# Setup loads moved from ScalarE's queue to SyncE's, and the own rows' factor of the second layer's softmax carried in scalars

## The chip, the cores and the metric

The kernel runs on one core of a Trainium2 chip. The metric is the device time of one execution in microseconds. The kernel before takes 4919.24 us (median of three runs, 4918.93 to 4925.36). One more execution was profiled; it took 4916.51 us, and its trace is the one read here.

## The reference

Four graph layers run one after the other over 6250 nodes of 256 numbers and 106250 edges sorted by target node. Each layer norms x, takes the positive part, does its own work and adds the result to x.

```python
edge_index = jnp.stack([src, dst])
h = jnp.maximum(_layernorm(x, axis=-1), 0.0)
x = x + _L0_gnn_ref(h, L0_gnn_weight, L0_gnn_bias, edge_index, edge_weight)
h = jnp.maximum(_layernorm(x, axis=-1), 0.0)
x = x + _L1_gnn_ref(h, edge_index, L1_gnn_W, L1_gnn_b, ...)
h = jnp.maximum(_layernorm(x, axis=-1), 0.0)
x = x + _L2_gnn_ref(h, edge_index, L2_gnn_W, L2_gnn_a)
h = jnp.maximum(_layernorm(x, axis=-1), 0.0)
x = x + _L3_gnn_ref(h, src, dst, L3_gnn_w_neigh, L3_gnn_w_self, L3_gnn_b_self)
```

The second layer (`_L1`) is the one whose end the change touches. It is a softmax over a node's incoming edges, to which the node's own row is added, and then a map into a ball:

```python
ex = jnp.exp(scores - mx[tgt])
se = jax.ops.segment_sum(ex, tgt, num_segments=N)
attn_weights = ex / (se[tgt] + 1e-10)
agg = jax.ops.segment_sum(h_src * attn_weights[:, None], tgt, num_segments=N)
h_combined = h + agg
h_poincare = _expmap0(h_combined)
norms = jnp.linalg.norm(h_poincare, axis=1, keepdims=True)
return jnp.where(norms > MAX_NORM, h_poincare * (MAX_NORM / (norms + 1e-08)), h_poincare)
```

`_expmap0(u)` is `tanh(|u|) * u / |u|`, so each row needs the sum of its squares.

## The kernel before

The nodes stand as 49 blocks of 128 rows (NB = 49), a block's 128 nodes on the 128 partitions; seven blocks are a part (UN = 7), seven parts are everything (OUTER = 7). X, H and A are three arrays of all 49 blocks in on-chip memory. The edges stand as 840 steps of 128. In each layer's pass GpSimd gathers 128 rows a step from a table in DRAM, TensorE multiplies them by a matrix of ones and zeros (or weights) that sorts them into a block's nodes, and VectorE adds the product to A. Between two passes come a norm of x, the layer's matrix product and the store of a new table in DRAM, and only when the last part of the table has landed does the next pass begin to gather.

Nothing plans the order: each engine's program is written out as one list (`block.sync`, `block.gpsimd`, `block.tensor`, `block.scalar`, `block.vector`), an engine runs its list in order, and semaphores join the lists. A DMA's issue stands in the list of the engine that issues it; what stands behind it waits until it has been issued.

**Setup.** x comes in as seven loads of a part each (`x_part(c)`, in ScalarE's list, L765; the last block's 106 rows apart, L776), src in three loads (L344 to L346, ScalarE), dst in three loads and seven more of single numbers (L344 to L354, SyncE), then SyncE loads a bias, the four weights (L358), the edge weights and small vectors (up to L367). VectorE takes the first part's statistics (`first_stats`, L1130 to L1139), ScalarE takes the roots (`root_first`, an Sqrt recorded at the helper's line L760), VectorE makes the norm's factor (`first_rstd`, L1144, L1145) and goes on to `fields` (L1152 to L1165), which packs dst and src into words and waits for `dst_in` at its head and `src_in` before its last line. Then statistics of the later parts alternate with seven moves of the words (L1170, L1172). ScalarE norms each part (H<-X) and squares five of the seven, VectorE the other two (L1214); SyncE stores the table part by part (L370); GpSimd's first gather (L484) waits for the whole table.

**Between second and third pass.** A holds the weighted sums of a softmax whose own rows are not in it yet. VectorE works out how the two parts are to be joined (`merge_gaps`, L1759 to L1767; two Exp on ScalarE; `merge_shares`, L1774 to L1780), all on 128x49 scalars. GpSimd multiplies each own row block in H by its share `be` (`scale_own`, L502, 49 blocks of 128x256), VectorE adds each to A times `kk` (`combine`, L1787), ScalarE squares each sum (`square_sum`, L760, A to a scratch part of wide_rows, sum into `aa`). VectorE then makes two columns of the next layer's weight (L2021), asks ScalarE for a Sqrt and a Tanh of the norm (L2024), ends with scalars in `t1` (L2025 to L2034), and adds A times `t1` to X block by block (`add_to_x`, L1697) as the first step of the next norm.

Of the kernel before, what the change touches and what calls it, by code (L numbers as in the profile page):

```python
# [56 lines left out]
MERGES = ((0, NB),)  # L57
# [24 lines left out]
def gnn_program(nc, x, src, dst, edge_weight, w0, bias0, w1, b1, mag_w, mag_b, attn_w, w2, a2,  # L82
                w_neigh, w_self, b_self, out):
    with ExitStack() as ctx:
# [262 lines left out]

        @block.sync
        def _(sp):
# [119 lines left out]
        def _(pool):  # L469
# [28 lines left out]
            def scale_own(lo, hi):  # L498

                pool.wait_ge(sem("shares"), len(MERGES))  # L500
                for b in range(lo, hi):
                    pool.tensor_scalar(H[:, b, 0:D], H[:, b, 0:D], col("be")[:, b:b + 1], None, ALU.mult).then_inc(sem("own_scaled_late"), 1)  # L502

# [251 lines left out]
        def _(act):  # L755
# [6 lines left out]
            def x_part(c):  # L762
                a, z = c * UN, min(c * UN + UN, NB - 1)
                act.sem_inc(sem("act_go"), 1)
                act.dma_start(X[:, a:z, :], x[a * P:z * P, :].rearrange("(b p) d -> p b d", p=P)).then_inc(sem(f"x_part{c}"), 16)  # L765
# [101 lines left out]
            def merge_parts(m):  # L867

                lo, hi = MERGES[m]
                act.wait_ge(sem("gaps"), m + 1)  # L870
                func(col("kk")[:, lo:hi], col("kk")[:, lo:hi], ACT.Exp)
                func(col("be")[:, lo:hi], col("be")[:, lo:hi], ACT.Exp).then_inc(sem("gap_exps"), 1)

            def scale_own(m, b):

                act.wait_ge(sem("shares"), m + 1)
                func(H[:, b, 0:D], H[:, b, 0:D], ACT.Identity, scale=col("be")[:, b:b + 1]).then_inc(sem("own_scaled"), 1)

            def merges(s):

                for m, (lo, hi) in enumerate(MERGES[:-1]):
                    at = s - (LT + hi)
                    if at == 4:
                        merge_parts(m)
                    if 0 <= at - 8 < hi - lo:
                        scale_own(m, lo + at - 8)
                    if 0 <= at - 14 < hi - lo:
                        square_sum(lo + at - 14)

            def weighted(q):  # L890
# [10 lines left out]
                def turn(i, last):  # L901
                    for h in range(2):
                        for k in range(GR):
# [6 lines left out]
                            if q == 0:  # L910
                                merges(s)
# [163 lines left out]
            for m, (lo, hi) in enumerate(MERGES[:-1]):  # L1075
                for b in range(max(lo, lo + S_REAL - LT - hi - 8), hi):
                    scale_own(m, b)
            merge_parts(len(MERGES) - 1)
            for m, (lo, hi) in enumerate(MERGES):
                for b in range(lo if m == len(MERGES) - 1 else max(lo, lo + S_REAL - LT - hi - 14), hi):  # L1080
                    square_sum(b)
# [15 lines left out]
        def _(dve):  # L1097
# [656 lines left out]
            def merge_gaps(m):  # L1754

                lo, hi = MERGES[m]
                z, peaks = A[:, lo:hi, AUX], A[:, lo:hi, AUX3]
                t2, t3, over, own = (col(name)[:, lo:hi] for name in ("t2", "t3", "kk", "be"))
# [5 lines left out]
                chain(tt(t3, H[:, lo:hi, AUX2], H[:, lo:hi, AUX3], ALU.max))  # L1764
                chain(tt(t3, t3, t2, ALU.max))
                tt(over, t2, t3, ALU.subtract)
                tt(own, H[:, lo:hi, AUX2], t3, ALU.subtract).then_inc(sem("gaps"), 1)  # L1767

            def merge_shares(m):

                lo, hi = MERGES[m]
                dve.wait_ge(sem("gap_exps"), m + 1)
                t2, over, own = (col(name)[:, lo:hi] for name in ("t2", "kk", "be"))
                chain(tt(t2, A[:, lo:hi, AUX], over, ALU.mult))  # L1774
# [14 lines left out]
            def merges(s):  # L1789

                for m, (lo, hi) in enumerate(MERGES[:-1]):
                    at = s - (LT + hi)
                    if at == 0:
                        merge_gaps(m)
                    if at == 6:
                        merge_shares(m)
# [300 lines left out]
```

## Time and profile before

| what | us |
|---|---|
| median of three runs | 4919.24 |
| the profiled execution's own time | 4916.51 |
| its span, first instruction to last | 4914.3 |
| VectorE busy | 3201.9 (65%) |
| GpSimd busy | 3237.7 (66%) |
| TensorE busy | 3102.4 (63%) |
| ScalarE busy | 1812.3 (37%) |

No engine is busy throughout, and none bounds the whole: the four passes and the stages between them have different limits. A row of the timeline reads: start, duration, engine (ACTq and SPq are the lists of ScalarE and SyncE where they issue DMAs), line, operation, what is written and read, how many, and in brackets how long the engine had been idle before and what ended that.

### The profile page before, as it was taken

What the parts mean: (1) busy time and instruction counts of PE and PEld (TensorE: products, weight loads), DVE (VectorE), ACT (ScalarE), POOL (GpSimd) and SP (SyncE); (2) the same over time, 40 slices, a digit from 0 to 9 for tenths busy, and PEclk for the clock granted to TensorE, in tenths of its full rate; (3) what the DMA queues carried; (4) which work ended last, traced back from release to release, by engine and by line L of the source; (5) the groups of instructions that cost most, each with busy time, mean ns of one, the idle gap of its engine ahead of it and who ended that gap; (6) DMA issues with size and microseconds to landing.
All of it is one profiled execution on the core that took longest, in us unless ns stands there. A gap on an engine that the chain in (4) does not pass through costs nothing. (4 is left out here: it accounts for less than half of the span.)

```text
span 4914.3 us, 56189 instructions
## 1 busy us (share of the span) xinstructions
PE 3102.4 (63%) x11120; PEld 2159.2 (44%) x11120; DVE 3201.9 (65%) x10216; ACT 1812.3 (37%) x4295; POOL 3237.7 (66%) x3382
## 2 busy tenths in 40 slices
PE   1788888885454666665545556656666666666665
PEld 1566666563332333333333444444443544444443
DVE  7999999999864666666676555555557544444445
ACT  4555555556872333333346433333336200000000
POOL 1777777773007777777762777777772577777776
PEclk6989999987776777777777787788887878778787
DMA  4544444443044333433334545445454544434434
GB/s 153 137 131 131 132 132 133 131 131 105 1 116 108 106 106 105 107 105 106 106 98 136 132 132 132 131 130 133 133 132 136 148 113 113 114 105 113 113 106 144
DMA packets 290664, 586.89 MB, mean 119 GB/s; under 512 B 63201, under 2 KB 170717, under 8 KB 290334
## 3 DMA queue, kind: packets, MB, share of 16 engines
q0 software_dynamic: 159456, 440.74, 33.8%
q1 hardware_dynamic: 99472, 108.21, 7.0%
q10 hardware_dynamic: 31406, 34.36, 2.5%
q8 instruction: 107, 1.75, 0.1%
q14 instruction: 223, 1.83, 0.1%
HBM read 530.98 MB, written 52.10 MB: 119 GB/s over the span
## 5 line engine op out<-in xcount | busy, mean ns | idle before, releaser
L494 POOL DMA_INDIRECT X<-table,src_tab x2490 | 2383.7, 957 | 1275.2 <-issue 715.2
L619 PE MATMUL psum<-X,onehot 128*128 128x259 f32 x4980 | 1726.1, 493 | 883.0 <-ACT onehot L760 365.5
L619 PEld LDWEIGHTS psum<-X,onehot 128*128 128x128 f32 x4980 | 1105.8, 241 | 1304.7 <-ACT onehot L760 537.2
L1305 DVE SCALAR_TENSOR_TENSOR A<-A,psum 128x259 f32 x1660 | 702.3, 423 | 665.5 <-PE psum L619 549.7
L484 POOL DMA_INDIRECT X<-table,src_tab x832 | 804.8, 967 | 348.7 <-issue 237.6
L760 ACT ACTIVATE onehot<-G,zero_col,ecols 128x128 f32<-128x128 bf16 x1660 | 686.8, 481 | 652.3 <-PE psum L619 504.4
L1305 DVE SCALAR_TENSOR_TENSOR A<-A,same_tab,psum 128x259 f32 x1620 | 775.3, 479 | 114.3 <-PE psum L619 12.3
L628 PE MATMUL psum<-H,G 128*128 x1664 | 571.0, 430 | 193.8 <-DVE G L1395 184.1
L606 PE MATMUL psum<-X,onehot 128*128 128x259 f32 x1664 | 539.6, 409 | 4.3 <-DVE A L1305 3.6
L628 PEld LDWEIGHTS psum<-H,G 128*128 128x128 f32 x1664 | 313.8, 208 | 349.9 <-issue 309.3
L760 ACT ACTIVATE ecols<-ecols,zero_col 128x20 f32<-128x20 f32 (+2 forms) x178 | 49.9, 302 | 931.0 <-DVE ecols L1871 455.4
L760 ACT ACTIVATE onehot<-onehot,zero_col,coef 128x128 f32<-128x128 bf16 x832 | 346.2, 481 | 115.1 <-DVE coef L1438 83.7
L1093 ACT COPY onehot<-psum 128x256 f32<-128x256 f32 x49 | 18.2, 372 | 970.4 <-PE psum L592 970.4
L1395 DVE SCALAR_TENSOR_TENSOR G<-psum,X 128x257 f32<-128x257 f32 x832 | 346.4, 417 | 41.3 <-DMA X<-table,src_tab 39.4
L606 PEld LDWEIGHTS psum<-X,onehot 128*128 128x128 f32 x1664 | 340.1, 206 | 70.4 <-issue 9.3
L1290 DVE TENSOR_TENSOR G<-psum,dst_tab 128x1280 bf16<-128x1280 f32 x168 | 249.4, 1485 | 38.6 <-ACT onehot L760 38.6
L1402 DVE TENSOR_SCALAR onehot<-iota_b,dst_tab 128x128 bf16<-128x128 bf16 x832 | 220.4, 265 | 0.0
L1865 DVE TENSOR_REDUCE ecols<-psum 128x20 f32<-128x60 f32 x42 | 9.2, 220 | 311.0 <-DMA X<-table,src_tab 311.0
L657 PE MATMUL psum<-ident,ecols 128*20 128x128 f32 x42 | 16.1, 383 | 289.7 <-DVE ecols L1703 289.6
L760 ACT ACT_TABLE_LOAD x131 | 168.1, 1283 | 44.6 <-issue 29.7
L1703 DVE COPY ecols<-X 128x20 f32<-128x20 f32 x42 | 7.4, 177 | 261.4 <-DMA X<-table,src_tab 261.4
L568 PE MATMUL psum<-ident,H 128*128 128x128 f32 x294 | 62.1, 296 | 164.1 <-ACT H L760 164.1
(375 smaller groups left out, 3083.2 us busy)
## 6 DMA issues: line engine op xcount, KB each, us to landing
X<-table,src_tab POOLq DMA_INDIRECT x3322, 2.8
plain<-rows_dram ACTq DMA_DIRECT2D x168, 160.0 KB, 3.3
plain<-rows_dram SPq DMA_DIRECT2D x104, 256.0 KB, 3.4
table<-H SPq DMA_DIRECT2D x21, 906.5 KB, 5.8
x_dram<-X SPq DMA_DIRECT2D x21, 896.0 KB, 4.1
X<-x_dram SPq DMA_DIRECT2D x14, 896.0 KB, 5.2
table<-A SPq DMA_DIRECT2D x7, 906.5 KB, 6.9
G<-x_dram SPq DMA_DIRECT2D x7, 896.0 KB, 5.6
```

Of the source, the lines that this page charges most:

```text
L484: pool.indirect_dma_start(ring0[:, s % SLOTS0, :], None, table, bass.IndirectOffsetOnAxis(src_tab[:, s:s + 1], 0)).then_inc(sem(f"batch0_{ ...
L494: pool.indirect_dma_start(ring[:, s % SLOTS, :], None, table, bass.IndirectOffsetOnAxis(src_tab[:, s:s + 1], 0)).then_inc(sem(f"batch_in{s ...
L568: ins = pe.transpose(turned[j % 4][:, c * P:c * P + P], source[:, b, c * P:c * P + P], ident[:, :])
L606: pe.matmul(psum[:, s % ACC_BANKS, 0:W], hots0[:, s % HOTS0, :], ring0[:, s % SLOTS0, :], start=True, stop=True).then_inc(sem("used"), 1)
L619: pe.matmul(psum[:, k % ACC_BANKS, 0:W], hots[:, k % HOTS, :], ring[:, k, :], start=True, stop=True).then_inc(sem("used"), 1)
L628: pe.matmul(psum[:, 4 + s % 4, 0:D + 1], oht[:, s // B0 % 2, s % B0, :], blk(H, at, 0, D + 1), start=True, stop=True).then_inc(sem("own_ro ...
L760: return act.activation(out_, in_, f, **kw)
L1093: act.copy(late_v, late_turned).then_inc(sem("late_kept"), 1)
L1290: return tt(out_, numbers.rearrange("p (o n) -> p o n", o=1).to_broadcast([P, n, P]), dst_tab[:, bass.ds(first, n)].rearrange("p (s o) -> ...
L1305: stt(total, total, same, psum[:, t % ACC_BANKS, 0:W], ALU.mult, ALU.add).then_inc(sem("sum_added"), 1)
L1395: stt(junk0[:, q, k % 2, at:at + D + 1], psum[:, 4 + s % 4, 0:D + 1], 1.0, ring0[:, s % SLOTS0, 0:D + 1], ALU.mult, ALU.mult, accum_out=en ...
L1402: ts(equal0[:, s % GR0, :], iota_b[:, :], dst_tab[:, s:s + 1], None, ALU.is_equal).then_inc(sem("equal_0"), 1)
```

## The change

Setup: `x_part` becomes a function that either list can call. ScalarE keeps the first part and src; SyncE issues parts 1 and 2 behind the bias and ahead of the weights, and parts 3 to 6 and the last block's rows behind the weights and ahead of the edge weights. ScalarE's wait for `dst_in` between the parts goes.

Between the passes: the joined row was `kk*A + be*H` with `be = 1 + own share`. Now the row is divided by `be`: `kk` is divided by it, the row is `kk*A + H`, and `be` is put back in scalars, its square into the sum of squares `aa` and itself into `t1`. GpSimd's 49 multiplications go. ScalarE squares blocks 0 to 35 (SQ_ACT = 36), VectorE squares blocks 36 to 48 between its own sums. The loops over MERGES, which had one entry, go too.

```diff
-MERGES = ((0, NB),)
+SQ_ACT = 36
...
+        def x_part(eng, c):
+            a, z = c * UN, min(c * UN + UN, NB - 1)
+            eng.dma_start(X[:, a:z, :], x[a * P:z * P, :].rearrange("(b p) d -> p b d", p=P)).then_inc(sem(f"x_part{c}"), 16)
...
+            x_part(sp, 1)
+            x_part(sp, 2)
             for n, w in enumerate((w0, w1, w_neigh, w_self)):
                 sp.dma_start(wraw[:, n], w.rearrange("(c p) d -> p c d", p=P)).then_inc(sem("raw_in"), 16)
+            for c in range(3, OUTER):
+                x_part(sp, c)
+            sp.wait_ge(sem("x_padded"), 1)
+            sp.dma_start(X[0:TAIL, NB - 1, :], x[(NB - 1) * P:N, :]).then_inc(sem(f"x_part{OUTER - 1}"), 16)
...
                 gathers(q)
-                if q == 0:
-                    scale_own(*MERGES[-1])
...
-            x_part(0)
+            act.sem_inc(sem("act_go"), 1)
+            x_part(act, 0)
             rows_in(act, src, src_rows_i, "src_padded", 1, "src_in")
-            x_part(1)
             act.sem_inc(sem("turned_kept"), 4)
             act.sem_inc(sem("coef_ready"), 2)
-            act.wait_ge(sem("dst_in"), 16 * (3 + EC))
-            for c in range(2, OUTER):
-                x_part(c)
-            act.wait_ge(sem("x_padded"), 1)
-            act.dma_start(X[0:TAIL, NB - 1, :], x[(NB - 1) * P:N, :]).then_inc(sem(f"x_part{OUTER - 1}"), 16)
...
+            merge_exps()
+            for b in range(SQ_ACT):
+                square_sum(b)
...
                 chain(ts(t2, t2, 1e-10, None, ALU.add))
-                chain(dve.reciprocal(t2, t2))
-                chain(tt(over, over, t2, ALU.mult))
+                chain(tt(own, own, t2, ALU.add))
+                chain(dve.reciprocal(own, own))
+                chain(tt(over, over, own, ALU.mult))
+                dve.reciprocal(t2, t2)
+                chain(dve.reciprocal(own, own))
                 chain(tt(own, own, t2, ALU.mult))
-                ts(own, own, 1.0, None, ALU.add).then_inc(sem("shares"), 1)
...
             def combine(b):
-                if b < MERGES[-1][0]:
-                    dve.wait_ge(sem("own_scaled"), b + 1)
-                else:
-                    dve.wait_ge(sem("own_scaled_late"), b - MERGES[-1][0] + 1)
                 stt(A[:, b, 0:D], A[:, b, 0:D], col("kk")[:, b:b + 1], H[:, b, 0:D], ALU.mult, ALU.add).then_inc(sem("combined"), 1)
...
+            def square_combined(b):
+                dve.wait_ge(sem("combined"), b + 1)
+                stt(junk[:, b % UN, :], A[:, b, 0:D], 1.0, A[:, b, 0:D], ALU.mult, ALU.mult,
+                    accum_out=col("aa")[:, b:b + 1]).then_inc(sem("squared_dve"), 1)
...
+            for b in range(NB):
                 combine(b)
+                if b > SQ_ACT:
+                    square_combined(b - 1)
+            square_combined(NB - 1)
...
-            dve.wait_ge(sem("squared"), 5 * NB)
+            tt(col("t4"), col("be"), col("be"), ALU.mult).then_inc(sem("share_square"), 1)
+            dve.wait_ge(sem("share_square"), 1)
+            dve.wait_ge(sem("squared_dve"), NB - SQ_ACT)
+            dve.wait_ge(sem("squared"), 4 * NB + SQ_ACT)
+            chain(tt(col("aa"), col("aa"), col("t4"), ALU.mult))
...
+            chain(tt(col("t1"), col("t1"), col("be"), ALU.mult))
```

ScalarE's list at the head of the program, before (L765 and L776 are the loads of x, L760 is every activation):

```order
L765 DMA X<-in_x 128x7x256
L344 DMA G<-in_src 128x6x128
L345 DMA G<-in_src 62x128
L346 DMA G<-in_src 1x10
L765 DMA X<-in_x 128x7x256 x5
L765 DMA X<-in_x 128x6x256
L776 DMA X<-in_x 106x256
L760 ACT_TABLE_LOAD
L760 ACTIVATE cols<-mv,tiny 128x7
```

The same place now (L350 is the load of a part of x, L762 every activation):

```order
L350 DMA X<-in_x 128x7x256
L344 DMA G<-in_src 128x6x128
L345 DMA G<-in_src 62x128
L346 DMA G<-in_src 1x10
L762 ACT_TABLE_LOAD
L762 ACTIVATE cols<-mv,tiny 128x7
```

Seven loads no longer stand between the src rows and the first activation. On SyncE they now stand here, from the single numbers of dst (L358) to the first edge weights (L344):

```order
L358 DMA G<-in_dst 128x1 x6
L358 DMA G<-in_dst 62x1
L360 DMA wide_rows<-in_L_gnn_bias 128x256
L350 DMA X<-in_x 128x7x256 x2
L364 DMA onehot<-in_L_gnn_weight 128x2x256
L364 DMA onehot<-in_L_gnn_W 128x2x256
L364 DMA onehot<-in_L_gnn_w_neigh 128x2x256
L364 DMA onehot<-in_L_gnn_w_self 128x2x256
L350 DMA X<-in_x 128x7x256 x3
L350 DMA X<-in_x 128x6x256
L368 DMA X<-in_x 106x256
L344 DMA A<-in_edge_weight 128x6x128
```

Both loads of dst stay ahead of every load of x on that list, and the edge weights come after the last. VectorE's list where the second layer's sums are joined, before (rows of cols are scalars of all 49 blocks; L1787 is `combine`, L2021 the weight's two columns):

```order
L1774 TENSOR_TENSOR cols<-A,cols 128x49
L1775 TENSOR_TENSOR cols<-cols 128x49
L1776 TENSOR_SCALAR cols<-cols 128x49
L1777 RECIPROCAL cols<-cols 128x49
L1778 TENSOR_TENSOR cols<-cols 128x49
L1779 TENSOR_TENSOR cols<-cols 128x49
L1780 TENSOR_SCALAR cols<-cols 128x49
L1787 SCALAR_TENSOR_TENSOR A<-A,cols,H 128x256 x49
L2021 SCALAR_TENSOR_TENSOR G,w2T<-w2T,wide_rows 128x256 x4
L2024 TENSOR_SCALAR cols<-cols 128x49
```

The same place now (L1752 is `combine`, L1756 a block's squares on VectorE):

```order
L1744 TENSOR_TENSOR cols<-cols 128x49
L1745 RECIPROCAL cols<-cols 128x49
L1746 TENSOR_TENSOR cols<-cols 128x49
L1747 RECIPROCAL cols<-cols 128x49
L1748 RECIPROCAL cols<-cols 128x49
L1749 TENSOR_TENSOR cols<-cols 128x49
L1752 SCALAR_TENSOR_TENSOR A<-A,cols,H 128x256 x38
L1756 SCALAR_TENSOR_TENSOR G,cols<-A 128x256
L1752 SCALAR_TENSOR_TENSOR A<-A,cols,H 128x256
...
L1979 SCALAR_TENSOR_TENSOR G,w2T<-w2T,wide_rows 128x256 x4
L1981 TENSOR_TENSOR cols<-cols 128x49
L1985 TENSOR_TENSOR cols<-cols 128x49
```

The scalars ahead of the sums are nine instead of seven; the 49 sums are still there, with 13 rows of squares between and behind the last of them; two more scalars stand ahead of the question to ScalarE, and one more (L1997) ahead of `add_to_x`.

## Rows read from the trace of the kernel before

**Rows 1.** Stretch, length, busy PE, PEld, DVE, ACT, POOL (instructions), clock, DMA share, GB/s.
```profile
0.00:31.50 31.50, 3.65 (x16) 3.27 (x16) 7.09 (x32) 1.58 (x2) 5.05 (x11) 0.88 0.99 296
...
2546.00:2603.00 57.00, 0.00 (x0) 0.00 (x0) 42.39 (x86) 34.51 (x105) 44.09 (x49) 0.53 0.14 46
...
2711.00:3760.00 1049.00, 637.97 (x2476) 431.05 (x2476) 557.87 (x1344) 375.32 (x940) 773.31 (x807) 0.80 0.50 131
```

**Rows 2.** Timeline of ScalarE, 0 to 32 us; then of 13 to 14 us alone.
```profile
3.04 0.99 ACTq L346 DMA_DIRECT2D G<-in_src  x1
4.14 23.26 ACTq L765 DMA_DIRECT2D X<-in_x  x6
...
30.98 0.30 ACT L760 ACTIVATE cols<-mv,tiny 128x7 f32<-128x7 f32 x1
...
13.67 0.40 ACTq L765 DMA_DIRECT2D X<-in_x  x1
```

**Rows 3.** Timeline of VectorE, 30 to 80 us.
```profile
31.31 0.20 DVE L1144 RECIPROCAL cols<-cols 128x7 f32<-128x7 f32 x1 [21.99 <-ACT cols L760]
...
31.63 1.08 DVE L1152 TENSOR_SCALAR G<-G 128x896 int32<-128x896 int32 x1
...
43.57 2.38 DVE L1130 BATCH_NORM_STATS2 G<-X 128x6 f32<-128x256 f32 x7
...
79.37 2.38 DVE L1130 BATCH_NORM_STATS2 G<-X 128x6 f32<-128x256 f32 x7
```

**Rows 4.** DMA of 7 to 12 us; ScalarE's queue: packets, MB, share of 16 engines.
```profile
DMA packets 2717, 1.47 MB, mean 294 GB/s; under 512 B 951, under 2 KB 2717, under 8 KB 2717
...
q10 hardware_dynamic: 1468, 1.17, 86.1%
```

**Rows 5.** Timeline of SyncE, 0 to 110 us; GpSimd's first gather.
```profile
50.52 45.12 SPq L370 DMA_DIRECT2D table<-H  x7
...
101.36 1.70 POOL L484 DMA_INDIRECT X<-table,src_tab  x1 [95.50 <-DMA table<-H]
```

**Rows 6.** Timeline of VectorE, 2549 to 2552 us.
```profile
2549.59 0.23 DVE L1774 TENSOR_TENSOR cols<-A,cols 128x49 f32<-128x49 f32 x1 [0.63 <-ACT cols L760]
...
2550.32 0.46 DVE L1777 RECIPROCAL cols<-cols 128x49 f32<-128x49 f32 x1
2550.82 0.21 DVE L1778 TENSOR_TENSOR cols<-cols 128x49 f32<-128x49 f32 x1
```

**Rows 7.** All instructions of L502, then of L1787 (min/median/max ns).
```profile
L502 POOL TENSOR_SCALAR H<-H,cols x49: 912/913/931, 2551.6 to 2594.8; 128x256 f32<-128x256 f32 x49
...
L1787 DVE SCALAR_TENSOR_TENSOR A<-A,cols,H x49: 484/695/701, 2552.6 to 2595.7; 128x256 f32<-128x256 f32 x49
```

**Rows 8.** Timeline of VectorE, 2595 to 2603 us.
```profile
2595.73 0.48 DVE L1787 SCALAR_TENSOR_TENSOR A<-A,cols,H 128x256 f32<-128x256 f32 x1 [0.20 <-POOL H L502]
2596.13 0.42 DVE L2021 SCALAR_TENSOR_TENSOR G<-w2T,wide_rows 128x256 f32<-128x256 f32 x1
...
2602.96 0.88 DVE L1697 SCALAR_TENSOR_TENSOR X<-A,cols,X 128x256 f32<-128x256 f32 x2
```

**Rows 9.** The like sums and squares elsewhere: VectorE at 1192 and 4904 us.
```profile
1192.00 0.48 DVE L1478 SCALAR_TENSOR_TENSOR A<-H,cols,A 128x256 f32<-128x256 f32 x1
1192.40 0.42 DVE L1481 SCALAR_TENSOR_TENSOR G<-H,A 128x256 f32<-128x256 f32 x1
...
1192.74 0.48 DVE L1478 SCALAR_TENSOR_TENSOR A<-H,cols,A 128x256 f32<-128x256 f32 x1
...
4904.07 3.26 DVE L1931 SCALAR_TENSOR_TENSOR H<-A,cols,H 128x256 f32<-128x256 f32 x8
```

**Rows 10.** ScalarE's squares back to back; SyncE's loads of x back.
```profile
46.96 0.49 ACT L760 ACTIVATE plain<-H,zero_col 128x256 f32<-128x256 f32 x1
...
47.45 0.49 ACT L760 ACTIVATE plain<-H,zero_col 128x256 f32<-128x256 f32 x1
...
2523.57 22.31 SPq L403 DMA_DIRECT2D X<-x_dram  x6
```

More of the change, by code:

```diff
@@ L496, in gathers @@
                                             ).then_inc(sem(f"batch_in{s // BATCH % (SLOTS // BATCH)}"), 16)
[L498 to L502, printed above, removed]
             pool.wait_ge(sem("src_kept"), 1)
@@ L865, in elu_parts, with merge_exps @@
                     func(H[:, b - 1, 0:D], H[:, b - 1, 0:D], ACT.Exp, scale=-1.0).then_inc(sem("elu_exp"), 1)
[L867 to L888, printed above, removed]
+            def merge_exps():
+                act.wait_ge(sem("gaps"), 1)
+                func(col("kk"), col("kk"), ACT.Exp)
+                func(col("be"), col("be"), ACT.Exp).then_inc(sem("gap_exps"), 1)
             def weighted(q):
@@ L909, in turn @@
                             weigh(q, i, h * GR + k)
-                            if q == 0:
-                                merges(s)
                             if q == 1 and s >= LT + ELU_LAG:
@@ L1074, in _ @@
             weighted(0)
[L1075 to L1081, printed above, removed]
+            merge_exps()
+            for b in range(SQ_ACT):
+                square_sum(b)
             asked(20)
@@ L1752, in fade_first, with merge_gaps @@
                 chain(stt(blk(A, at, AUX3, W), blk(A, at, AUX, AUX + 1), drop, blk(A, at, AUX3, W), ALU.mult, ALU.add))
[L1754 to L1758, printed above, removed]
+            def merge_gaps():
+                z, peaks = A[:, :, AUX], A[:, :, AUX3]
+                t2, t3, over, own = (col(name) for name in ("t2", "t3", "kk", "be"))
                 ts(t3, z, 0.5, -BIG, ALU.is_lt, ALU.mult)
@@ L1763, in merge_gaps @@
                 chain(tt(t2, t2, t3, ALU.add))
-                chain(tt(t3, H[:, lo:hi, AUX2], H[:, lo:hi, AUX3], ALU.max))
+                chain(tt(t3, H[:, :, AUX2], H[:, :, AUX3], ALU.max))
                 chain(tt(t3, t3, t2, ALU.max))
                 tt(over, t2, t3, ALU.subtract)
[L1767 to L1774, printed above, removed]
+                tt(own, H[:, :, AUX2], t3, ALU.subtract).then_inc(sem("gaps"), 1)
@@ L1775, in merge_shares @@
+            def merge_shares():
+                dve.wait_ge(sem("gap_exps"), 1)
+                t2, over, own = (col(name) for name in ("t2", "kk", "be"))
+                chain(tt(t2, A[:, :, AUX], over, ALU.mult))
                 chain(tt(t2, t2, own, ALU.add))
                 chain(ts(t2, t2, 1e-10, None, ALU.add))
-                chain(dve.reciprocal(t2, t2))
-                chain(tt(over, over, t2, ALU.mult))
+                chain(tt(own, own, t2, ALU.add))
[3 more added lines that the diff above has]
+                chain(dve.reciprocal(own, own))
@@ L1779, in merge_shares @@
                 chain(tt(own, own, t2, ALU.mult))
-                ts(own, own, 1.0, None, ALU.add).then_inc(sem("shares"), 1)
             def combine(b):
-                if b < MERGES[-1][0]:
-                    dve.wait_ge(sem("own_scaled"), b + 1)
-                else:
-                    dve.wait_ge(sem("own_scaled_late"), b - MERGES[-1][0] + 1)
                 stt(A[:, b, 0:D], A[:, b, 0:D], col("kk")[:, b:b + 1], H[:, b, 0:D], ALU.mult, ALU.add).then_inc(sem("combined"), 1)
[L1789 to L1796, printed above, removed]
-                    if 0 <= at - 10 < hi - lo:
-                        combine(lo + at - 10)
+            def square_combined(b):
+                dve.wait_ge(sem("combined"), b + 1)
+                stt(junk[:, b % UN, :], A[:, b, 0:D], 1.0, A[:, b, 0:D], ALU.mult, ALU.mult,
+                    accum_out=col("aa")[:, b:b + 1]).then_inc(sem("squared_dve"), 1)
@@ L1819, in turn @@
                             add_sum(0, i, h * GR + k, at[k], same_g[:, h:h + 1] if k == 0 else None)
-                            merges(s)
                             if last and h:
@@ L2009, in _ @@
             softmax_sums()
-            merge_gaps(len(MERGES) - 1)
-            for m, (lo, hi) in enumerate(MERGES[:-1]):
-                for b in range(max(lo, lo + S_REAL - LT - hi - 10), hi):
-                    combine(b)
-            merge_shares(len(MERGES) - 1)
-            for b in range(*MERGES[-1]):
+            merge_gaps()
+            merge_shares()
+            for b in range(NB):
                 combine(b)
+                if b > SQ_ACT:
+                    square_combined(b - 1)
+            square_combined(NB - 1)
             dve.wait_ge(sem("vectors_in"), 16 * 5)
```

4 lines of the change are left out of this document (removed).

## The prediction, made before the changed kernel was run

> **What bounds the kernel now.** I read the busy times by stage first, then the timelines of the two stages that the change touches. In the first 31.5 us VectorE is busy 7.09 us while the DMA engines are busy 0.99 of the time [rows 1]. VectorE is not waiting for data, though: at 31.31 it ends an idle time of 21.99 us, released by ScalarE's root [rows 3]. That root runs at 30.98 because ScalarE's list has to issue its loads of x first, six of them from 4.14 to 27.40 [rows 2]. A reader is to see that a load's issue, not its arrival, holds the engine. From there to the first gather at 101.36 us, which waits for the table's last store [rows 5], the way is VectorE's list: `fields` at 31.63, the second part's statistics right behind it at 43.57, the last part's at 79.37 [rows 3]. An earlier `fields` therefore brings an earlier first gather.
>
> Between the second and third pass TensorE does nothing for 57 us; GpSimd is busy 44.09 us of them [rows 1]. Its 49 multiplications take 913 ns each and every `combine` on VectorE follows one of them [rows 7]; the last one starts at 2595.73 [rows 8]. So GpSimd's pace bounds that stretch.
>
> **The setup, part by part.** Without the seven loads ScalarE's issues end at 4.03 [rows 2]. Its table load and root then wait for VectorE's variances, which are there at 31.31 - 21.99 = 9.32. The root takes 0.3, the reciprocal starts 0.33 after the root starts and `fields` 0.32 after that [rows 2, 3]: `fields` can start at 10.0 at the earliest, 21.6 us ahead of 31.63.
>
> It also waits for `dst_in`. Before, ScalarE waited for the same semaphore ahead of part 2 and went on at 13.67 [rows 2]; dst stands ahead of every x on SyncE's list and is issued as before, so 13.67 is the other end: 18.0 us. Which is nearer? From 7 to 12 us ScalarE's queue moved 1.17 MB (part 1 and the end of src) while 951 packets under 512 B, mostly dst's single numbers, went beside it [rows 4]. Part 1 is 0.92 MB (128 x 7 x 256 numbers), 3.1 us at 294 GB/s, and stands behind dst now. Some two thirds to three quarters of that should come off 13.67; I take 11.3, a gain of 20.3 us. The Trainium skill, "DMA: Bandwidth & Descriptors", section Queues, rings and completion order, says that each DMA engine goes round the queue rows that have work, a packet at a time. By that rule the single numbers no longer share turns with part 1, and the gain is nearer 21.6 (1.3 us less than my sum); if the queues did not share turns it is 18.0. The rows on two queues side by side in 7 to 12 us agree with the rule, but not how much is given back.
>
> Next late could be x. Part 1 is needed 11.94 us after `fields` starts (43.57 - 31.63), at 23.3; part 6 at 79.37 - 20.3 = 59.1 [rows 3]. All loads together took until about the end of the 31.5 us at 296 GB/s [rows 1], and bytes do not change; part 1 stands behind dst and a bias only. So it is there. SyncE's list pays for the issues now: 23.26 us for six at the pace of the data [rows 2]. Queued behind them are the edge weights, the vectors and the table's stores. The first store, 50.52 before [rows 5], would be ready at 30.2 and may be issued some us late, but only the last store counts, 95 before and 75 now, long after the loads. Edge weights and vectors are read near the first gather. Cost 0. Sum of the setup: -20.3 us, ends -18.0 and -21.6.
>
> **The join, part by part.** Removed: 49 multiplications on GpSimd, and one scalar row and VectorE's wait for GpSimd. Scalars: a chained one takes 0.24 us (three from 2549.59 to 2550.32) and a reciprocal 0.50 (2550.32 to 2550.82) [rows 6]. The first three end 0.73 after 2549.59; then an addition, a reciprocal, a product, two reciprocals, a product: 0.73 + 3 x 0.24 + 3 x 0.50 = 2.95. The first `combine` starts at 2552.5, where it started at 2552.6 before [rows 7]: nothing.
>
> The 49 sums: with GpSimd at work one takes 0.695 us and the pace is GpSimd's; the last one, alone, takes 0.48 [rows 7, 8]. The same operation on the same kinds of operands runs eight in 3.26 us at the end of the kernel, a pace of (3.26 - 0.48) / 7 = 0.397 [rows 9]. A sum and a square with accumulator in turn, both fp32 from on-chip memory, take 0.74 for the pair at 1192 us, so a square 0.345 [rows 9]. New: 37 x 0.397 + 12 x 0.74 + 0.35 = 23.9 us. VectorE reaches the weight's columns (L2021) at 2552.5 + 24.0 = 2576.5, before 2596.13 [rows 8]: -19.6. Ends: 0.70 for each sum if it were slow by itself, 49 x 0.30 = 14.8 us worse; 0.345 for each, 2.6 better.
>
> ScalarE's 36 squares at 0.49 [rows 10] take 17.6 from the first sum's end at 2552.9, to 2570.6, beside VectorE and 6 us before it is done. Above 0.65 a square they would set the end. Added on the path: two scalars ahead of ScalarE's root and one ahead of `add_to_x`, 3 x 0.24 = 0.7. Next late could be x's way back from DRAM: SyncE has issued its loads by 2523.57 + 22.31 = 2545.9 [rows 10], nearly 40 us before `add_to_x` at 2602.96 - 18.9 = 2584.1 [rows 8]. The sum of the join: -19.6 + 0.7 = -18.9 us, ends -4.1 and -21.5.
>
> The Trainium skill, "Vector Engine (DVE) Microarchitecture Reference", section Points that are easy to get wrong, speaks against this change: a scalar-tensor-tensor with two non-bf16 on-chip sources runs at half throughput. At two cycles an element and the 0.96 GHz of "VectorE: DVE Perf Modes" (Specifications) that would be an estimate of 0.53 us for each of 62, 33 us for the join's loop, and a gain of 9.9 instead of 18.9. The paces of 0.397 and 0.345 for just these operands [rows 9] are below that, so the trace does not bear it out here, and I go by the rows.
>
> **Sum.** -20.3 - 18.9 = -39.2 us. The profiled execution took 4916.51 (span 4914.3 and 2.2 around it), so 4877.3 in its terms; the median of the runs is 2.7 above it, 4919.24, so 4880.0. Nothing after either place depends on when it starts: the passes follow their tables.
>
> **The rivals.** (a) The sums stay at 0.70 each without GpSimd, being slow on their own operands: for it, 48 of 49 rows; against it, the 49th (0.48) and the rows at 4904 [rows 7 to 9]. The join gives 4.1, the time is 4895. (b) The loads on one queue arrive late: statistics wait for x on VectorE. For it, the DMA engines are busy 0.99 in that stretch [rows 1]; against it, 20 us of slack at part 6. It decides once part 6 lands after 59.1; with 10 of the setup's 20 us lost the time is 4890. The variant that the edits of the setup don't act, because something else holds the root, is 4900; the rows show nothing else ahead of the root. (c) Slower: with 39 us of idle gone TensorE is granted a lower clock in the passes. A pass ran at 0.80 of 2.4 GHz, between the two levels of 1.2 and 2.4, with 638 us of matmuls in 1049, GpSimd 773 [rows 1]. Three such passes hold some 1900 us of matmuls; were all of them on the path, a clock lower by 2% would take the 39 us back, and by 3% make it slower by 18 us, 4937. Matmuls that GpSimd's gathers hide count nothing, so it needs more than that; and the stretch that shortens has a granted clock of 0.53 anyway [rows 1].
>
> **How the numbers follow.** Forecast 4880: 0.82, its own range 4873 to 4889 (ends of `dst_in`, the sums' pace, and the 6 us that the runs differ). (a) 0.05, (b) and its variant 0.08, (c) 0.03, anything else 0.02. Both good ends together give 4919.24 - 21.6 - 21.5 = 4876, and a run may fall a few us below; (a) and (b) reach 4890 to 4900. A range of 4871 to 4894 leaves out less than 2 in 10. A measurement tells 0.2% (9.8 us) from no change: all cases but (c) and part of the rest are faster by more, so faster 0.94, same 0.04, slower 0.02.
>
> **What would show it.** Right: ScalarE's first root near 9.4, `fields` near 11 (wrong if after 13.7), first gather near 81; no multiplication on GpSimd, sums 0.40 apart, the next layer's `add_to_x` 38 to 40 us earlier in the span, and the passes as long as before. Wrong: statistics of parts 1 to 6 idle behind a load; sums 0.70 apart; ScalarE's squares ending after VectorE's; passes two and three longer.

## The result, and the profile after

The changed kernel takes 4843.31 us (median, 4842.31 to 4844.75), the kernel before on the same chip 4919.09 us (4918.35 to 4925.36): a ratio of 0.9843, 95% interval 0.9826 to 0.9860, so 75.8 us less where 39.2 were predicted. The profiled execution took 4844.75 us, its span is 4842.9.

The setup first. Timeline of ScalarE after the change, 0 to 32 us, against [rows 2]:

```profile
3.06 0.86 ACTq L346 DMA_DIRECT2D G<-in_src  x1
9.39 1.28 ACT L762 ACT_TABLE_LOAD   x1 [9.39 <-DVE mv L1108]
10.69 0.30 ACT L762 ACTIVATE cols<-mv,tiny 128x7 f32<-128x7 f32 x1
```

And VectorE's of the same stretch, against [rows 3]:

```profile
11.02 0.20 DVE L1113 RECIPROCAL cols<-cols 128x7 f32<-128x7 f32 x1 [1.71 <-ACT cols L762]
...
11.84 1.09 DVE L1121 TENSOR_SCALAR G<-G 128x896 int32<-128x896 int32 x1 [0.42 <-DMA G<-in_dst]
```

ScalarE's issues end at 3.92; the root waits for the variances (9.39), and its table load runs only after that wait, so the root is at 10.69 instead of 30.98. `fields` starts at 11.84 instead of 31.63, and dst's arrival ends its wait, the last 0.42 us of it: the root and dst, the two that it waits for, come within half a microsecond of each other. SyncE's timeline, then GpSimd's first gather, against [rows 5]:

```profile
14.08 8.19 SPq L350 DMA_DIRECT2D X<-in_x  x4
...
32.87 42.99 SPq L380 DMA_DIRECT2D table<-H  x7
```

```profile
82.58 2.03 POOL L494 DMA_INDIRECT X<-table,src_tab  x1 [76.72 <-DMA table<-H]
```

The first gather comes 101.36 - 82.58 = 18.8 us earlier (in 13 later profiles of kernels with the new setup it starts at 81.3 to 82.2). The loads of x cost SyncE nothing that counts: VectorE never waits for x, and the last part's statistics start at 59.59 (79.37 before).

Then the join. Timeline of VectorE from the scalars to the next layer's first update, against [rows 6 and 8]; behind it all instructions of the sums' line and of the squares' line (min/median/max ns), against [rows 7]:

```profile
2513.61 0.23 DVE L1741 TENSOR_TENSOR cols<-A,cols 128x49 f32<-128x49 f32 x1 [0.63 <-ACT cols L762]
...
2516.15 0.21 DVE L1749 TENSOR_TENSOR cols<-cols 128x49 f32<-128x49 f32 x1
...
2538.46 0.48 DVE L1752 SCALAR_TENSOR_TENSOR A<-A,cols,H 128x256 f32<-128x256 f32 x1
2538.86 0.42 DVE L1756 SCALAR_TENSOR_TENSOR G<-A 128x256 f32<-128x256 f32 x1
2539.20 0.08 DVE L1756 DVE_READ_ACCUMULATOR G<-A 128x1 f32 x1
2539.20 0.48 DVE L1752 SCALAR_TENSOR_TENSOR A<-A,cols,H 128x256 f32<-128x256 f32 x1
...
2540.29 0.42 DVE L1979 SCALAR_TENSOR_TENSOR G<-w2T,wide_rows 128x256 f32<-128x256 f32 x1
...
2547.88 0.88 DVE L1666 SCALAR_TENSOR_TENSOR X<-A,cols,X 128x256 f32<-128x256 f32 x2
```

```profile
L1752 DVE SCALAR_TENSOR_TENSOR A<-A,cols,H x49: 479/482/489, 2516.4 to 2539.2; 128x256 f32<-128x256 f32 x49
...
L1756 DVE SCALAR_TENSOR_TENSOR G<-A x13: 418/422/426, 2531.4 to 2539.9; 128x256 f32<-128x256 f32 x13
```

A sum and a square take 2539.20 - 2538.46 = 0.74, a sum alone 0.40, the paces of [rows 9], and the loop 2516.40 to 2540.29 = 23.9 us; from the first sum to `add_to_x` there are 31.5 us where there were 50.4. ScalarE's last square, against [rows 10], is done 5.6 us before VectorE's:

```profile
2516.92 0.51 ACT L762 ACTIVATE wide_rows<-A,zero_col 128x256 f32<-128x256 f32 x1 [3.34 <-DVE A L1752]
...
2534.14 0.49 ACT L762 ACTIVATE wide_rows<-A,zero_col 128x256 f32<-128x256 f32 x1
...
2534.74 1.28 ACT L762 ACT_TABLE_LOAD   x1
```

So far 18.8 + 18.9 = 37.7 of the 75.8 us; 38 are still to be found. They are in the passes. How much earlier the same gather starts after the change:

| gather | earlier by, us |
|---|---|
| the first, setup done | 18.8 |
| the last of layer 0's pass | 28.9 |
| second pass, first and last | 27.3, 36.1 |
| third pass (the join lies ahead of it), first and last | 55.5, 64.0 |
| fourth pass, first and last | 63.6, 71.8 |

Every pass gained 8 to 10 us, layer 0's as well, in which neither part of the join has run yet. GpSimd's groups by line (operation, count, busy us, mean ns), of the kernel before:

```profile
L494 POOL DMA_INDIRECT X<-table,src_tab x2490 | 2383.7, 957 | 1275.2 <-issue 715.2 <-DMA table<-H 397.3 <-DMA table<-A 120.4
L484 POOL DMA_INDIRECT X<-table,src_tab x832 | 804.8, 967 | 348.7 <-issue 237.6 <-DMA table<-H 95.5 <-PE psum L606 15.5
```

and of the changed one:

```profile
L504 POOL DMA_INDIRECT X<-table,src_tab x2490 | 2358.1, 947 | 1336.3 <-issue 705.1 <-DMA table<-H 457.9 <-DMA table<-A 120.8
L494 POOL DMA_INDIRECT X<-table,src_tab x832 | 794.7, 955 | 329.9 <-issue 234.9 <-DMA table<-H 76.7 <-PE psum L608 18.3
```

3322 gathers are busy 3188.5 us before and 3152.8 after: 35.7 us, some 11 ns each. The median is 957 ns before and 946 after, the shortest 952 and 940; the median pause from one gather to the next is 305 ns in both. 18.8 + 18.9 + 35.7 = 73.4 us, where the spans differ by 71.4 (some 2 us are given back between passes, see the table) and the medians by 75.8. By stage, against [rows 1] (the pass in its new place):

```profile
0.00:31.50 31.50, 3.65 (x16) 3.27 (x16) 26.35 (x64) 9.67 (x26) 5.06 (x11) 1.00 0.93 281
2509.00:2547.00 38.00, 0.00 (x0) 0.00 (x0) 33.98 (x115) 22.89 (x79) 0.00 (x0) 0.56 0.22 72
2655.00:3696.00 1041.00, 636.80 (x2476) 430.96 (x2476) 562.34 (x1344) 375.89 (x941) 765.31 (x807) 0.80 0.50 132
```

In these stretches of the third pass the same 807 gathers are busy 765.31 us instead of 773.31, and the pass from its first gather to its last takes 1039.2 us instead of 1047.7, with the granted clock at 0.80 as before. The gathers and their 305 ns pauses fill some 1011 of the 1041 us: GpSimd's gathers set the pass's length. What made a gather shorter, with the gather itself unchanged, was the question of the experiments.

### The profile page after: what moved, and what is told of

Read it like the earlier page. It is cut to its first block and busy times, and to the rows that moved or that the text cites. A ratio compares the mean times of both kernels' runs of the same rounds, so it can differ in the third digit from the quotient of the medians.

```text
span 4842.9 us, 56126 instructions
## 1 busy us (share of the span) xinstructions
PE 3094.3 (64%) x11120; PEld 2149.0 (44%) x11120; DVE 3195.8 (66%) x10247; ACT 1800.2 (37%) x4269; POOL 3157.9 (65%) x3333
## 5 line engine op out<-in xcount | busy, mean ns | idle before, releaser
L504 POOL DMA_INDIRECT X<-table,src_tab x2490 | 2358.1, 947 | 1336.3 <-issue 705.1
L494 POOL DMA_INDIRECT X<-table,src_tab x832 | 794.7, 955 | 329.9 <-issue 234.9
L762 ACT ACTIVATE onehot<-G,zero_col,ecols 128x128 f32<-128x128 bf16 x1660 | 686.4, 481 | 646.4 <-PE psum L621 512.8
L762 ACT ACTIVATE ecols<-ecols,zero_col 128x20 f32<-128x20 f32 (+2 forms) x178 | 49.9, 302 | 912.8 <-DVE ecols L1829 444.9
L762 ACT ACTIVATE onehot<-onehot,zero_col,coef 128x128 f32<-128x128 bf16 x832 | 346.0, 481 | 115.5 <-DVE coef L1407 88.7
L1259 DVE TENSOR_TENSOR onehot<-psum,dst_tab 128x640 f32<-128x640 f32 x166 | 135.9, 819 | 44.1 <-issue 35.0
```

Source lines behind the costliest of these rows:

```text
L494: pool.indirect_dma_start(ring0[:, s % SLOTS0, :], None, table, bass.IndirectOffsetOnAxis(src_tab[:, s:s + 1], 0)).then_inc(sem(f"batch0_{ ...
L504: pool.indirect_dma_start(ring[:, s % SLOTS, :], None, table, bass.IndirectOffsetOnAxis(src_tab[:, s:s + 1], 0)).then_inc(sem(f"batch_in{s ...
L762: return act.activation(out_, in_, f, **kw)
L1259: return tt(out_, numbers.rearrange("p (o n) -> p o n", o=1).to_broadcast([P, n, P]), dst_tab[:, bass.ds(first, n)].rearrange("p (s o) -> ...
```

## The experiments

Theory A: GpSimd's multiplications, which the change took out of its list, made each gather longer. Rivals: B, the setup's new order did it; C, something else that differs between the programs (numbers of semaphores, the other engines' lists in the join). The median gather of a profile is the reading; times stand beside it.

**e1_setup_only**: the kernel before with the setup's edits alone (SyncE issues parts 1 to 6).

```diff
+            x_part(sp, 1)
+            x_part(sp, 2)
...
-            x_part(1)
```

> The kernel before with the setup's edits alone; GpSimd keeps its 49 multiplications. All theories: first gather at 82 to 83 us instead of 101.4. Theory A (a gather takes 946 instead of 957 ns because GpSimd's program no longer holds the multiplications): gathers stay at 957 ns, time 4919 - 19 = 4900. Theory B (the gathers' pace comes with the setup's edits, for example with the semaphores' numbers): 946 ns, time near 4919 - 19 - 35 = 4865. Theory C (the pace differs from one compiled program to the next for no reason in either edit): neither value can be foretold, it need not be 946 or 957.

4899.21 us beside 4921.9, ratio 0.9958 (0.9944 to 0.9972); first gather at 81.51 us, gathers 957 ns. The setup is worth 22.7 us by the medians, and does nothing to the gathers: B falls.

**e2_join_only**: the changed kernel with the old setup, so the join's edits alone.

```diff
-            x_part(sp, 1)
-            x_part(sp, 2)
...
+            x_part(1)
```

> The changed kernel with the setup of before: the join's edits alone, no multiplications on GpSimd. All theories: the stretch between passes two and three 19 to 20 us shorter. Theory A: gathers at 946 ns, time near 4919 - 20 - 35 = 4864. Theory B: 957 ns, time near 4899. Theory C: any value.

4868.21 us, ratio 0.9892 (0.9876 to 0.9909); gathers 946 ns. 53.7 us from the join's edits, 18.9 of them in the join (31.5 us from the first sum to `add_to_x`, as in the changed kernel). The two parts add up to 22.7 + 53.7 = 76.4, but only to within some 10 us: e2's runs reach from 4859.09, the profiled one, to 4868.93.

**e3_after_one_mul**: the changed kernel with one multiplication on GpSimd between the second and the third pass.

```diff
                 gathers(q)
+                if q == 0:
+                    pool.tensor_scalar(coef[:, 0, :], coef[:, 0, :], iota_part[:, 0:1], None, ALU.mult)
```

> The changed kernel with one small multiplication (128x16, by a column) on GpSimd between the second layer's gathers and the third's, whose result nobody reads. Theory A: gathers back at 957 ns from the first layer on, time near 4843 + 35 = 4878. Theory B: 946 ns, 4843 to 4845. Theory C: any value.

4846.49 us, ratio 0.9847 (0.9830 to 0.9863); gathers 947 ns. One such instruction (128x16) isn't enough, so theory A, which gave 957 ns to it, failed as it stood.

**e4_before_sems**: the kernel before with its semaphores numbered as in the changed one.

```diff
+        for name in ("dst_padded", "dst_in", "bias_in", "x_part1", ...):
+            sem(name)
```

> The kernel before with the names of its first semaphores taken in the order of the changed kernel, so that most semaphores have the changed kernel's numbers; not one instruction moves. Theory A: gathers at 957 ns, 4919. Theory B in its form that the numbers count: 946 ns, near 4884. Theory C: any value.

4921.91 us, ratio 1.000 (0.999 to 1.001); gathers 957 ns. Not the numbers.

**e5_49_muls, e6_49_muls_end, e8_24_muls**: the changed kernel with multiplications of 128x1 numbers that nobody reads. e5 has 49 where the old ones stood, e8 24 there, e6 49 behind the last gather.

```diff
                 gathers(q)
+                if q == 0:
+                    for b in range(49):
+                        pool.tensor_scalar(col("xa")[:, b:b + 1], iota_node[:, 0:1], iota_part[:, 0:1], None, ALU.mult)
```

Expected of e5:

> The changed kernel with 49 multiplications on GpSimd again, at the place of the old ones (ahead of the third pass's gathers), but of 128x1 numbers that nobody reads and without a wait. Theory 'number of instructions': the length of GpSimd's program sets what each gather takes; median gather 957 ns again in all passes, the time 4843 + some 32 us of slower gathers + at most 49 x 0.1-0.2 = 5 to 10 us for the multiplications, 4875 to 4890. Theory 'these multiplications' (their size, operands or waits): gathers stay at 946 ns, 4848 to 4856. Theory 'another part of the join's edits' (lists of VectorE or ScalarE): 946 ns, 4848 to 4856.

Expected of e6:

> The changed kernel with the same 49 unread multiplications at the very end of GpSimd's list, behind the last gather. They run beside nothing that the end waits for (some 600 us of work of other engines? at least the last rows' sums), so they cost nothing themselves. Theory 'number of instructions': gathers of all passes 957 ns although the multiplications come after them, 4875 to 4880. The two other theories: 946 ns, 4843 to 4846.

Expected of e8:

> The changed kernel with 24 of the unread multiplications ahead of the third pass's gathers. Theory 'number of instructions': gathers between 946 and 957 ns if the duration grows with the list's length, 957 or 946 if a threshold decides; 4843 + 0 to 37 us. The two other theories: 946 ns, 4846 to 4850.

e5: 4879.64 us, ratio 0.9925 (0.9902 to 0.9947). e8: 4879.13, ratio 0.9924 (0.9896 to 0.9953). e6: 4846.96, ratio 0.9859 (0.9824 to 0.9894). GpSimd's groups in e5:

```profile
L504 POOL DMA_INDIRECT X<-table,src_tab x2490 | 2385.9, 958 | 1320.1 <-issue 714.0 <-DMA table<-H 443.8 <-DMA table<-A 118.6
L494 POOL DMA_INDIRECT X<-table,src_tab x832 | 806.2, 969 | 329.5 <-issue 237.0 <-DMA table<-H 76.3 <-PE psum L611 16.1
L516 POOL TENSOR_SCALAR cols<-iota_node,iota_part 128x1 f32<-128x1 f32 x49 | 12.5, 275 | 0.0
```

12.5 us of small multiplications make the gathers 3192.1 - 3152.8 = 39.3 us busier, those ahead of them as those behind, and the kernel 36 us longer by the medians (40 by what each gains over the kernel before on its own chip, 75.8 and 36.0), with nothing of the join undone. In e6 the same 49 leave the gathers at 949 (its two runs took 4839.66 and 4854.25): "the number of instructions" falls, and so does the expected growth with the number (24 do what 49 do).

**e7_scale_on_act**: the kernel before with its 49 multiplications on ScalarE.

```diff
-                if q == 0:
-                    scale_own(*MERGES[-1])
...
+                    if b < hi:
+                        scale_own(m, b)
```

> The kernel before with its 49 multiplications of the own rows moved from GpSimd to ScalarE (128x256 each, ahead of the squares; VectorE's and ScalarE's lists are otherwise those of before). Theories 'number of instructions' and 'these multiplications': GpSimd's list is that of the changed kernel, so gathers take 946 ns, 33 us or more below 4919 from the passes, and the join is bound by ScalarE (two operations of about 0.45 a row, some 45 us as before): 4880 to 4890. Theory 'another part of the join's edits': gathers stay at 957 ns, 4915 to 4922.

4885.29 us, ratio 0.9944 (0.9921 to 0.9966); gathers 949 ns, with VectorE's and ScalarE's other work in the join as before and the join itself no shorter (53.7 us from the first sum to `add_to_x`, 50.4 before). C falls: it is the multiplications on GpSimd.

**e9_8_muls, e15_3_muls**: e5 with 8 and with 3 of them. **e10_49_memsets, e13_49_tensor_tensor, e14_49_copies**: e5 with another operation. **e11_49_muls_late, e16_muls_last_gather, e12_49_muls_first**: 49 of them between the third and the fourth pass, directly ahead of the last gather, and ahead of the first. The lines that differ from e5's, shortened:

```diff
e9, e15: range(8), range(3)
e10: pool.memset(col("xa")[:, b:b + 1], 0.0)
e13: pool.tensor_tensor(col("xa")[:, b:b + 1], iota_node[:, 0:1], iota_part[:, 0:1], ALU.mult)
e14: pool.tensor_copy(col("xa")[:, b:b + 1], iota_node[:, 0:1])
e11: if q == 1:
e16: if q == 2 and s == S_REAL - 1:   (in gathers, ahead of the gather)
e12: the loop of e5 ahead of gathers_layer0(), into a tile of its own
```

Expected of e9:

> The changed kernel with 8 unread 128x1 multiplications on GpSimd between the second and the third pass (24 there gave gathers of 957 ns, one gave 947). Theory 'dose': the median gather lies between, 948 to 955 ns, 4850 to 4870 us. Theory 'threshold' : 946 to 949 or 957 ns, 4843 to 4855 or 4877 to 4881 us.

Expected of e15:

> The changed kernel with three of the unread multiplications between the second and the third pass. Theory 'threshold by number': 946 to 949 ns (threshold above 3, 4840 to 4855 us) or 957 ns (between 1 and 3, 4875 to 4882 us). Theory 'dose': between 949 and 956 ns, some 4855 to 4870 us.

Expected of e10:

> The changed kernel with 49 memsets of 128x1 in the place of the 49 unread multiplications. Theory 'any instruction between the passes': gathers take 957 ns, 4875 to 4882 us. Theory 'multiplications alone': 946 to 949 ns, 4843 to 4855 us.

Expected of e13:

> The changed kernel with 49 unread 128x1 tensor-tensor multiplications on GpSimd between the second and the third pass. Theory 'any arithmetic between gathers': gathers 957 ns, 4875 to 4882 us. Theory 'the tensor-scalar operation alone': 946 to 949 ns, 4840 to 4855 us.

Expected of e14:

> The changed kernel with 49 unread 128x1 copies on GpSimd in the same place. Theory 'any arithmetic, or whatever reads a tile': gathers 957 ns, 4875 to 4882 us. Theory 'the tensor-scalar operation alone': 946 to 949 ns, as with memsets, 4840 to 4855 us.

Expected of e11:

> The changed kernel with the 49 unread multiplications between the third and the fourth pass instead of between the second and the third. Theory 'gathers follow them in the list': 957 ns in all passes, 4875 to 4882 us. Theory 'their place in the list matters': another value, between 946 and 957 ns.

Expected of e16:

> The changed kernel with the 49 unread multiplications directly ahead of the very last gather, where they cost up to some 15 us themselves. Theory 'gathers on both sides' (whatever their number): gathers of all passes 957 ns, 4880 to 4895 us. Theory 'a run of gathers has to follow': 946 to 949 ns, 4843 to 4865 us.

Expected of e12:

> The changed kernel with the 49 unread multiplications ahead of the first gather, where GpSimd waits for the table anyway. Theory 'gathers follow them in the list': 957 ns in all passes, 4875 to 4882 us. Theory 'multiplications between gathers': 946 to 949 ns, 4843 to 4855 us.

These eight are single runs; the gathers tell them apart, 946 to 949 ns or 957 and nothing between. With the runs above:

| kernel | on GpSimd besides gathers | where | median gather, ns | us |
|---|---|---|---|---|
| before | 49 tensor-scalar 128x256 | between passes 2 and 3 | 957 | 4919.09 |
| e5, e8, e9 | 49, 24, 8 tensor-scalar 128x1 | same | 957, 957, 957 | 4879.64, 4879.13, 4879.06 |
| e15 | 3 tensor-scalar 128x1 | same | 957 | 4878.81 |
| e11 | 49 tensor-scalar 128x1 | between passes 3 and 4 | 957 | 4879.62 |
| e16 | 49 tensor-scalar 128x1 | ahead of the last gather | 957 | 4891.42 |
| e6 | 49 tensor-scalar 128x1 | behind the last gather | 949 | 4846.96 |
| e12 | 49 tensor-scalar 128x1 | ahead of the first gather | 946 | 4859.92 |
| e3 | 1 tensor-scalar 128x16 | between passes 2 and 3 | 947 | 4846.49 |
| e10 | 49 memsets 128x1 | same | 946 | 4839.98 |
| e13 | 49 tensor-tensor 128x1 | same | 946 | 4837.19 |
| e14 | 49 copies 128x1 | same | 946 | 4844.39 |

(e12's multiplications run after the table has landed, 22.4 us ahead of the first gather, and e16's 13.5 us ahead of the last; these stand in their times.) Three instructions of 0.3 us cost 34 to 42 us beside e14 and e13, which ran on the same chip; 49 tensor-tensor multiplications of the same numbers leave the gathers at 946 ns. All instructions of the gathers' two lines in e15 (min/median/max ns):

```profile
L494 POOL DMA_INDIRECT X<-table,src_tab x832: 952/957/1808, 81.6 to 1139.7; - x167
...
L504 POOL DMA_INDIRECT X<-table,src_tab x2490: 952/957/1392, 1452.4 to 4858.8; - x192
```

and in e13:

```profile
L494 POOL DMA_INDIRECT X<-table,src_tab x832: 942/946/1715, 82.2 to 1128.5; - x167
...
L504 POOL DMA_INDIRECT X<-table,src_tab x2490: 942/946/1156, 1439.5 to 4816.0; - x192
```

The shortest gather shifts with the median, and the median is the same in each of the four passes (957 in e15, 946 in e13). So no stretch escapes it, and nothing in these rows makes it come and go with the neighbours' work.

**e18_before_tensor_tensor**: the test on the real kernel. The kernel before, its 49 multiplications written as tensor-tensor operations.

```diff
-                    pool.tensor_scalar(H[:, b, 0:D], H[:, b, 0:D], col("be")[:, b:b + 1], None, ALU.mult)...
+                    pool.tensor_tensor(H[:, b, 0:D], H[:, b, 0:D], col("be")[:, b:b + 1].to_broadcast([P, D]), ALU.mult)...
```

> The kernel before with its 49 multiplications on GpSimd written as tensor-tensor operations (the row by its factor, broadcast along the row) instead of tensor-scalar ones; nothing else differs. Theory 'the tensor-scalar operation between gathers': gathers 946 ns in all passes, 33 to 36 us less from the passes, and the join as before or up to 10 us either way if the operation takes another time than 913 ns: 4875 to 4895 us. Theory 'these multiplications, whatever the operation': gathers 957 ns, 4910 to 4930 us.

4883.39 us beside 4925.97, ratio 0.9917 (0.9903 to 0.9930): a gain as large as the prediction gave to the whole change, from one operation written as another. Its groups on GpSimd:

```profile
L494 POOL DMA_INDIRECT X<-table,src_tab x2490 | 2366.5, 950 | 1272.8 <-issue 705.5 <-DMA table<-H 396.1 <-DMA table<-A 118.4
L484 POOL DMA_INDIRECT X<-table,src_tab x832 | 796.6, 957 | 349.4 <-issue 233.8 <-DMA table<-H 96.1 <-PE psum L606 19.5
L502 POOL TENSOR_TENSOR H<-H,cols 128x256 f32<-128x256 f32 x49 | 36.5, 782 | 34.2 <-DVE cols L1780 34.2
```

3188.5 - 3163.1 = 25.4 us come from the gathers, whose median is 949 ns: less than the 33 to 36 us that were expected with 946. The sums, from the first start to the last, take 2573.1 - 2537.0 = 36.1 us instead of 43.1 [rows 7], another 7.0. That is 32.4 of the 34.4 us between the profiled spans (4914.3 and 4879.9); the rest of the 42.6 is that the kernel before ran 9.5 us longer beside this one than in its profile (4925.97 and 4916.51), and this one 1.3 longer.

**e17_rebalanced**: the changed kernel with ScalarE's idle end of the join used.

```diff
-SQ_ACT = 36
+SQ_ACT = 43
...
-            scalar_func(ts(col("f0"), col("aa"), MIN_NORM ** 2, None, ALU.max))
+            ask(ts(col("f0"), col("aa"), MIN_NORM ** 2, None, ALU.max))
+            for c in range(2):
...
+            answered()
```

> The changed kernel with 43 squares on ScalarE instead of 36 and the four columns of the weight (1.87 us) computed while VectorE waits 2.05 us for ScalarE's root and tanh. Its trace shows VectorE's loop ending 5 to 6 us after ScalarE's squares, so 7 squares moved give 7 x 0.345 = 2.4 us and the columns 1.9: 4.3 us less, 4839 us, if the end of the loop sets the start of the next layer. If ScalarE's squares end the wait instead, 2 us or less. Gathers 946 ns in both.

4849.96 us beside 4925.97, ratio 0.9846 (0.9833 to 0.9860), where 4839 was expected: not told apart from the changed kernel's 0.9843. In its trace the way from the first sum to `add_to_x` is 28.2 us instead of 31.5, 3.3 of the expected 4.3. VectorE's timeline, then ScalarE's:

```profile
2519.34 17.91 DVE L1752 SCALAR_TENSOR_TENSOR A<-A,cols,H 128x256 f32<-128x256 f32 x45
...
2547.49 0.88 DVE L1666 SCALAR_TENSOR_TENSOR X<-A,cols,X 128x256 f32<-128x256 f32 x2
```

```profile
2540.52 0.49 ACT L762 ACTIVATE wide_rows<-A,zero_col 128x256 f32<-128x256 f32 x1
2540.92 0.18 ACT L762 ACTIVATION_READ_ACCUMULATOR wide_rows<-A,zero_col 128x1 f32 x1
2541.12 1.28 ACT L762 ACT_TABLE_LOAD   x1
2542.42 0.34 ACT L762 ACTIVATE cols<-cols,zero_col 128x49 f32<-128x49 f32 x1
```

With its squares done as late as VectorE's, ScalarE's table load of 1.28 us, which is over at 2536.0 in the changed kernel, moves onto the path. And this profile's gathers took 949 ns where 946 was expected, 10 us over 3322 of them: a difference as large as what was to be shown. So no version here is measurably better than the changed kernel.

## Why the prediction was wrong

**Setup: right, 18.8 us for 20.3.** `fields` at 11.84 for 11.3 and the root at 10.69 for 9.4: the table load, taken as done before the variances, waited with the root. That the sum hardly felt this 1.3 us is luck: dst landed 0.42 us after what hangs on the root was done. `fields` gained 19.8 us, between the ends of 18.0 and 21.6, which settles nothing on how the DMA queues share their turns. From the end of part 6's norm (70.33, 19.8 us earlier) to the first gather it took 1.0 us longer. Nothing waited for x. Rival (b) is out.

**Join: right in each term.** Scalars 2.8 us for 2.95, loop 23.9 for 23.9, ScalarE's squares done in 17.7 for 17.6, and from the first sum to `add_to_x` 18.9 us less, as predicted; the third pass's first gather gained another 19.4 on the second pass's last. Rival (a) is out: sums that took 0.695 beside GpSimd take 0.482, 0.40 apart. The prediction's 0.53 us a sum, 2.1 ns an element, is its own reading of a halved throughput, and the rows don't bear that reading out: VectorE's setup in the changed kernel has, next to each other,

```profile
14.04 0.62 DVE L1124 TENSOR_SCALAR A<-G 128x896 int32<-128x896 int32 x1
14.70 1.09 DVE L1125 SCALAR_TENSOR_TENSOR A<-G,A 128x896 int32<-128x896 int32 x1
```

The form with two sources takes 1.2 ns an element, and not quite twice what the row with one source takes. A throughput that is half of that row's fits the rows; 2.1 ns an element does not.

**Clock: right.** The pass is granted 0.80 as before, the whole kernel 0.807 (0.797 in the profile before, 0.795 to 0.809 in its other runs in e1 and e17): rival (c) is out.

**The sum: wrong, by its closing sentence.** "Nothing after either place depends on when it starts: the passes follow their tables", and so "the passes as long as before". The passes do follow their tables, and each is shorter. The step that failed lies earlier in the working: "Removed: 49 multiplications on GpSimd" was priced only where they stood, by the time they kept VectorE waiting, and what their removal does to the gathers was put at nothing without a row for it. That term measured 35.7 us, paid by 3322 other instructions of the same engine. Three experiments show it independently, each in the gathers' busy time: e5 (put back, 39.3 us more), e7 (moved away, 24.1 less) and e18 (written as another operation, 25.4 less). No row of the trace before shows it, since a gather's 957 ns has nothing beside it there to be long against; but no row excluded it either, and the range left no room for a list's effect on the rest of its engine.

**What stays open.** Shown is the condition: three or more tensor-scalar operations with gathers ahead of them and at least one behind; and that a memset, a copy or a tensor-tensor operation in the same place does nothing. Not shown is what in GpSimd does it. It isn't a state that the multiplications leave behind within one execution, since gathers ahead of them are as slow as those behind. Something of it is there from the start: the last of GpSimd's first four memsets, 0.33 us into the span, takes 118 ns in the changed kernel (its group by line),

```profile
L2051 POOL MEMSET const-uint8-127<- 128x1 uint8 x1 | 0.1, 118 | 0.0
```

and 101 before; 101 to 103 in all 12 kernels that have a tensor-scalar operation on GpSimd anywhere, 118 to 120 in the eight that have none. So something that goes with the operation is there before any of them has run in this execution, whether by what is loaded with the program or by what an earlier execution left; the runs don't tell which. And the memsets part the kernels otherwise than the gathers do: e3, e6 and e12 have short memsets and short gathers. Whether one instruction fails to do it for its number or its shape wasn't tried, nor whether e12's 49 fail to for their place alone, since they also write a tile of their own. Nor is it known why kernels with the shorter gathers show 946 or 947 ns in some profiles and 949 in others. The four at 949 (e6, e7, e17, e18) come from two chips on which no profile of the experiments shows 946, but the runs of e6 on one of them lie 14.6 us apart, more than 3 ns over 3322 gathers.

## What to carry to other kernels

When an instruction leaves an engine's list, compare the durations of everything else on that engine in the two traces, form by form, before looking for waits: here nearly half the gain was an 11 ns shift of a group's median and minimum, visible in one row. Where GpSimd mostly gathers, as here, it is worth trying to write a tensor-scalar operation between gathers as a tensor-tensor one, or to move it to another engine, and one look at the median gather says whether it paid. A load that only has to be issued belongs on a list with nothing urgent behind it, and one read of who waits for that list settles it.

## What the runs showed of the hardware

A gather of 128 rows took 957 or 946 to 949 ns by what else stood in GpSimd's list, as above. The Trainium skill, "GPSIMD Engine Reference", section 2.1 Instruction dispatch, has each instruction find its operation's entry in a table and call it, at a cost of its own. In these runs the price falls on other instructions, the gathers; no run shows whether it arises at that step.

VectorE's sum of 128x256 reads two tiles. It took 482 ns with GpSimd idle (485 in e7, where ScalarE multiplies the rows), 695 beside GpSimd's tensor-scalar multiplications [rows 7] and 829 beside the tensor-tensor ones; all instructions of that line in e18:

```profile
L1787 DVE SCALAR_TENSOR_TENSOR A<-A,cols,H x49: 473/829/833, 2537.0 to 2573.1; 128x256 f32<-128x256 f32 x49
```

The Trainium skill, "SBUF — State Buffer", section Who interferes with whom, says that a VectorE instruction with two inputs in on-chip memory contends with a GpSimd instruction that reads there. The runs agree, and add a size: 213 ns more beside the tensor-scalar operations and 347 beside the tensor-tensor ones.
